# Experts of a gated cross-attention block: the lower part of each weight on VectorE in quarters, GpSimd left with the row additions

## The chip, the cores and the metric

The kernel runs on one core of a Trainium2 chip. The metric is the device time of one execution in microseconds (us). A core has five engines that run their own instruction streams and meet at semaphores: TensorE (PE in the profile; PEld is its weight load), VectorE (DVE), ScalarE (ACT), GpSimd (POOL) and SyncE (SP), which issues DMAs here.

## The reference

The block computes `x + tanh(g) * xattn(layernorm(x))` and then `x + tanh(g) * ffn(layernorm(x))`. The change touches the second, a mixture of experts:

```python
B, S, D, F, E = (4, 512, 256, 1024, 8)           # here x is (8, 512, 256): 4096 tokens
capacity = max(int(N / E * 1.25), 1)              # 640 rows for an expert and a rank
router_probs = softmax(x_flat @ gate_w.T)
top_k_probs, top_k_idx = top_k(router_probs, 2)   # then normalized to a sum of 1
for k in range(2):
    ...
    disp = zeros((E, capacity, D)).at[eid, pos_c].add(where(valid, x_flat, 0))
    gate = silu(einsum('ecd,efd->ecf', disp, wi_gate))
    up = einsum('ecd,efd->ecf', disp, wi_up)
    expert_out = einsum('ecf,edf->ecd', gate * up, wo)
    out = out + where(valid, ew * expert_out[eid, pos_c], 0)
```

## The kernel before, in words

The program has five stages one after the other: `project`, `attend`, `repair`, `route` and `experts`. The first four compute the attention, the router and the rows' places, and write every expert's rows to a buffer in HBM (`scr_disp`). Only `experts` is touched; it runs from about 2475 us to the end of the span.

**Tiling.** The 2 x 640 rows of an expert are 5 chunks of 256 (`NCH` = 5, `R` = 256), 40 chunks in all, counted by `C`; `c` is the chunk within expert `e`. The hidden width F of 1024 is cut in 8 feature blocks of 128 (`FB` = 8).

**Two parts for each number.** TensorE multiplies in fp32r, so every fp32 operand is held as a rounded higher part and a lower part, the difference, and each product is three matmuls: lower x higher, higher x lower, higher x higher (L1467 to L1469). For the rows these are `e_xh` and `e_xl`, for the hidden values `e_hh` and `e_hl`, for the weights `e_wh` and `e_wl`. A weight (gate, up or down: `n` = 0, 1, 2) is 128 x 2048 values; `e_wh` and `e_wl` have two sets, one for the expert that runs and one for the next.

**A chunk, by engine.**
- TensorE transposes the chunk's rows into `e_ps_x` (L1459, 4 transposes), then does `down` of the chunk two before (48 matmuls into `e_ps_y`), then `up` of this chunk: for each feature block 12 matmuls into one of four banks `e_ps_gu`. Block f waits until `e_h` of block f-4 is done, as that frees its bank. Ahead of an expert's first chunk it waits until the three lower parts of its weights are done (`w_cut`).
- ScalarE rounds the rows (`e_xh`), weighs the results of the chunk two before (`e_y`, L1535) and takes tanh of each block (`e_th`).
- VectorE forms `e_xl` (L1546), and for each block `e_sg` (L1578), `e_hh` of the block before (L1551), `e_h` (L1587) and `e_hl` of the block before (L1555). In the last three chunks of an expert it also forms the higher part of one weight of the next, right behind `e_xl` (`high_weight`, L1563). Most of its experts run in a hardware loop over r, two experts an iteration; the other engines' code is unrolled.
- GpSimd adds the weighed rows of chunk `C` to the output with two indirect DMAs (`add_rows`, L1402), and forms the lower part of the weights (`cut_weight`, L1394), one 128 x 2048 subtraction each. The order is written out: chunk by chunk, first `add_rows(C - 2)`, then in the last three chunks of an expert one `cut_weight` for the next.
- SP loads weights into two buffers `e_raw` (`load_weight`, L1426) and rows into four buffers `e_xin` (`load_rows`, L1432). The load of a weight waits until the weight two before it is cut, since that frees the buffer.

Before the first chunk all three weights of expert 0 are loaded, rounded and cut; this is called the head below.

Of the kernel before, what the change touches and what calls it, by code (L numbers as in the profile page):

```python
# [5 lines left out]
F32 = mybir.dt.float32  # L6
# [4 lines left out]
ALU = mybir.AluOpType  # L11
# [3 lines left out]
P = 128  # L15
# [1315 lines left out]
def experts(nc, pl, io, scr, out):  # L1331
# [3 lines left out]
    D, E, F, KD, CAP = pl.D, pl.E, pl.F, pl.KD, pl.CAP  # L1335
    FB = F // P
    RT = 2 if (2 * CAP) % (2 * P) == 0 else 1
    R = RT * P
    NCH = 2 * CAP // R
    DX, XB, LATE = pl.DX, 4, 2  # L1340
    assert CAP % P == 0
    with ExitStack() as ctx:
        sb = lambda name, shape, dt=F32: ctx.enter_context(nc.sbuf_tensor(name, shape, dt))
        psum = lambda name, cols=512: ctx.enter_context(nc.psum_tensor(name, [P, cols], F32))
# [3 lines left out]
        raw = sb("e_raw", [P, 2, KD * F])  # L1348
# [22 lines left out]
        w_high = sem("e_w_high")  # L1371
# [12 lines left out]
        @block.gpsimd  # L1384
        def _(pool):
            nc.gpsimd.memset(ident[:], 0.0).then_inc(id0, 1)
            pool.wait_ge(id0, 1)
            nc.gpsimd.affine_select(out=ident[:], in_=ident[:], compare_op=ALU.not_equal, fill=1.0, base=0,
                                    pattern=[[-1, P]], channel_multiplier=1).then_inc(ident_ready, 1)

            def cut_weight(e, n):
                u = e % 2
                pool.wait_ge(w_high, 3 * e + n + 1)
                nc.gpsimd.tensor_tensor(wl[:, u, n], raw[:, (u + n) % 2], wh[:, u, n].bitcast(F32), ALU.subtract  # L1394
                                        ).then_inc(w_cut, 1)

            def add_rows(C):
                pool.wait_ge(y_sb, RT * (C + 1))
                if C:
                    pool.wait_ge(added, 16 * RT * C)  # L1400
                for r in range(RT):
                    pool.indirect_dma_start(  # L1402
                        out=out.rearrange("b s d -> (b s) d"),
                        out_offset=bass.IndirectOffsetOnAxis(ap=xin[:, C % XB, r, DX - 1:DX].bitcast(U32), axis=0),
                        in_=y[:, C % 2, r, :], in_offset=None, bounds_check=pl.N - 1, oob_is_err=False,
                        compute_op=ALU.add).then_inc(added, 16)

            for n in range(3):
                cut_weight(0, n)
            for C in range(E * NCH):  # L1410
                e, c = divmod(C, NCH)
                if C >= LATE:
                    add_rows(C - LATE)
                if c >= NCH - 3 and e + 1 < E:
                    cut_weight(e + 1, c - NCH + 3)
            for C in range(E * NCH - LATE, E * NCH):
                add_rows(C)
            pool.wait_ge(added, 16 * RT * E * NCH)

        @block.sync  # L1420
        def _(sp):
            def load_weight(e, n):
                u, name = e % 2, ("wgT", "wuT", "wdT")[n]
                if 3 * e + n >= 2:
                    sp.wait_ge(w_cut, 3 * e + n - 1)
                sp.dma_start(raw[:, (u + n) % 2, :].rearrange("p (k f) -> p k f", k=FB if n == 2 else KD),  # L1426
                             io[name][e].rearrange("(k p) f -> p k f", p=P)).then_inc(raw_in[(u + n) % 2], 16)

            def load_rows(C):
                if C >= XB:  # L1430
                    sp.wait_ge(added, 16 * RT * (C - XB + 1))
                sp.dma_start(xin[:, C % XB], scr["disp_c"][C].rearrange("(r p) d -> p r d", p=P)).then_inc(x_in[C % XB], 16)  # L1432

            for n in range(2):
                load_weight(0, n)
            load_rows(0)
            load_weight(0, 2)
            for C in range(E * NCH):
                e, c = divmod(C, NCH)
                if C:  # L1440
                    load_rows(C)
                if e + 1 < E and c == 0:
                    load_weight(e + 1, 0)
                    load_weight(e + 1, 1)
                if e + 1 < E and c == NCH - 1:
                    load_weight(e + 1, 2)

        @block.tensor
        def _(pe):
            pe.wait_ge(ident_ready, 1)  # L1450

            def turn(C, first):

                pe.wait_ge(x_in[C % XB], 16 * (C // XB + 1))
                if not first:
                    pe.wait_ge(x_cut, C)
                for k in range(KD):
                    for r in range(RT):
                        mm = nc.tensor.transpose(ps_x[:, k * R + r * P:k * R + (r + 1) * P],  # L1459
                                                 xin[:, C % XB, r, k * P:(k + 1) * P], ident[:])  # L1460
                mm.then_inc(x_turned, 1)

            def product(out, parts_a, parts_b):

                n = len(parts_a)
                for k, ((ah, al), (bh, bl)) in enumerate(zip(parts_a, parts_b)):
                    nc.tensor.matmul(out, al, bh, start=(k == 0), stop=False)  # L1467
                    nc.tensor.matmul(out, ah, bl, start=False, stop=False)  # L1468
                    mm = nc.tensor.matmul(out, ah, bh, start=False, stop=(k == n - 1))  # L1469
                return mm  # L1470

            def up(C, s, u, start):
                pe.wait_ge(x_cut, C + 1)
                for f in range(FB):
                    n = C * FB + f
                    if not (start and f < 4):
                        pe.wait_ge(h_done, n - 3)
                    for i in range(2):
                        part = [slice(k * F + f * P, k * F + (f + 1) * P) for k in range(KD)]
                        mm = product(ps_gu[f % 4][:, i * R:(i + 1) * R],  # L1480
                                     [(wh[:, u, i, c], wl[:, u, i, c]) for c in part],
                                     [(xh[:, s, k, :], xl[:, s, k, :]) for k in range(KD)])
                    mm.then_inc(gu_full, 1)

            def down(C, s, u, start):
                if not start:
                    pe.wait_ge(y_sb, RT * (C - 1))
                pe.wait_ge(h_cut, (C + 1) * FB)
                for r in range(RT):
                    rows = slice(r * P, (r + 1) * P)  # L1490
                    mm = product(ps_y[s][:, r * D:(r + 1) * D],
                                 [(hh[:, s, f, rows], hl[:, s, f, rows]) for f in range(FB)],
                                 [(wh[:, u, 2, f * D:(f + 1) * D], wl[:, u, 2, f * D:(f + 1) * D]) for f in range(FB)])
                mm.then_inc(y_full, 1)

            def expert(e, u, start):
                pe.wait_ge(w_cut, 3 * e + 3)
                for c in range(NCH):
                    C, q = e * NCH + c, u * NCH + c
                    s = q % 2  # L1500
                    turn(C, start and q == 0)
                    if not (start and q < 2):
                        down(C - 2, s, u if c >= 2 else 1 - u, start and q < 4)
                    up(C, s, u, start and q == 0)

            over(pe, E, 2, expert)
            for q in (2 * NCH - 2, 2 * NCH - 1):
                down((E - 2) * NCH + q, q % 2, 1, False)
# [34 lines left out]
        def _(dve):  # L1543
# [5 lines left out]
            def high(n, s, f):  # L1549
                dve.wait_ge(h_done, n + 1)  # L1550
                nc.vector.tensor_copy(hh[:, s, f, :], h[:, f % 2, :]).then_inc(h_high, 1)  # L1551

            def lower(n, s, f):
                dve.wait_ge(h_high, n + 1)
                nc.vector.tensor_tensor(hl[:, s, f, :], h[:, f % 2, :], hh[:, s, f, :].bitcast(F32), ALU.subtract  # L1555
                                        ).then_inc(h_cut, 1)

            def high_weight(e, u, n, start):
# [3 lines left out]
                    dve.wait_ge(y_full, NCH * (e - 1))  # L1562
                nc.vector.tensor_copy(wh[:, u, n], raw[:, (u + n) % 2]).then_inc(w_high, 1)  # L1563

            def expert(e, u, start, last=False):
                for c in range(NCH):
                    C, q = e * NCH + c, u * NCH + c
                    s = q % 2
                    cut_x(C, s)
                    if c >= NCH - 3 and not last:  # L1570
                        high_weight(e + 1, 1 - u, c - NCH + 3, start and u == 0)
                    for f in range(FB):
                        n = C * FB + f
# [14 lines left out]
                                                       in1=ps_gu[f % 4][:, R:2 * R], op0=ALU.mult, op1=ALU.mult).then_inc(h_done, 1)  # L1588
                        if f:
                            lower(n - 1, s, f - 1)  # L1590
                    high(C * FB + FB - 1, s, FB - 1)
                    lower(C * FB + FB - 1, s, FB - 1)


            for n in range(3):
                high_weight(0, 0, n, True)
            expert(0, 0, True)
            expert(1, 1, True)
            expert(2, 0, False)
# [90 lines left out]
```

## Time and profile before

| what | value |
|---|---|
| three runs | 3287.62 us median (3280.4 to 3288.7) |
| the profiled execution | 3283.47 us, its span 3281.7 us |
| PE busy | 2536.3 us, 77% of the span |
| DVE busy | 2788.9 us, 85% |
| ACT busy | 1460.3 us, 44% |
| POOL busy | 1915.2 us, 58% |
| mean granted TensorE clock | 0.914 of full speed |

Busy times are sums over the whole span, the four earlier stages included. In the rows further down, times are microseconds from the span's start unless a column is named ns; `L` and a number is a line of the kernel; `out<-in` names the tiles that an instruction writes and reads. A duration is the time from an instruction's start to its end; instructions that follow one another on an engine overlap a little, so start to start is shorter than the duration.

### The profile page before, as it was taken

What the parts mean: (1) busy time and instruction counts of PE and PEld (TensorE: products, weight loads), DVE (VectorE), ACT (ScalarE), POOL (GpSimd) and SP (SyncE); (2) the same over time, 40 slices, a digit from 0 to 9 for tenths busy, and PEclk for the clock granted to TensorE, in tenths of its full rate; (3) what the DMA queues carried; (4) which work ended last, traced back from release to release, by engine and by line L of the source; (5) the groups of instructions that cost most, each with busy time, mean ns of one, the idle gap of its engine ahead of it and who ended that gap; (6) DMA issues with size and microseconds to landing.
All of it is one profiled execution on the core that took longest, in us unless ns stands there. A gap on an engine that the chain in (4) does not pass through costs nothing. (4 is left out here: it accounts for less than half of the span.)

```text
span 3281.7 us, 64952 instructions
## 1 busy us (share of the span) xinstructions
PE 2536.3 (77%) x17723; PEld 1599.8 (49%) x17724; DVE 2788.9 (85%) x20206; ACT 1460.3 (44%) x1991; POOL 1915.2 (58%) x1393
## 2 busy tenths in 40 slices
PE   7837787887787778787788778753645999999998
PEld 4512333333333333333333333322544999999998
DVE  6739999999999999999999999956554777777775
ACT  2205666666666666666666666631111222222222
POOL 1017888888888888888888888840163233232231
PEclk9968999999999999999999999985767999999999
DMA  6961211212112112112121121101232222222221
GB/s 189 260 185 31 64 37 31 61 37 45 48 37 64 29 37 64 29 41 59 29 56 45 29 64 37 29 12 41 89 115 93 61 64 62 52 57 62 50 40 20
DMA packets 131053, 201.23 MB, mean 61 GB/s; under 512 B 22816, under 2 KB 97824, under 8 KB 127616
## 3 DMA queue, kind: packets, MB, share of 16 engines
q1 hardware_dynamic: 112768, 167.56, 18.9%
q0 software_dynamic: 17920, 29.52, 4.3%
q8 instruction: 141, 2.31, 0.3%
q14 instruction: 224, 1.84, 0.2%
HBM read 129.60 MB, written 69.50 MB: 61 GB/s over the span
## 5 line engine op out<-in xcount | busy, mean ns | idle before, releaser
L568 DVE MAX8 a_cand<-a_sc 128x8 f32<-128x43 f32 (+1 forms) x12288 | 1646.0, 193 | 50.3 <-ACT a_sc L509 50.2
L670 POOL TENSOR_SCALAR a_side<-a_sc,a_top 128x1024 bf16<-128x1024 f32 x512 | 1455.9, 2844 | 333.1 <-DVE a_top L602 329.4
L509 ACT COPY a_sc<-a_ps_s 128x1024 f32<-128x1024 f32 x512 | 518.3, 1012 | 781.2 <-POOL a_side L670 720.4
L520 ACT ACTIVATE a_pT<-a_ps_e 128x1024 f32<-128x1024 f32 x512 | 526.3, 1028 | 15.2 <-PE a_ps_e L440 11.4
L419 PE MATMUL a_ps_s<-a_ks,a_qs 96*128 96x512 bf16 x1024 | 319.6, 395 | 246.1 <-ACT a_sc L509 192.5
L433 PE MATMUL a_ps_e<-a_qs,a_ks 99*128 99x512 bf16 x1024 | 317.0, 392 | 179.5 <-ACT a_pT L520 178.6
L1402 POOL DMA_INDIRECT out<-e_y,e_xin x80 | 124.0, 1550 | 558.9 <-ACT e_y L1535 516.4
L472 PE MATMUL a_ps_o<-a_pT,a_vs 128*32 128x512 f32 x2048 | 429.0, 693 | 1.1 <-ACT a_pT L520 1.1
L1467 PE MATMUL e_ps_gu<-e_xh,e_wl 128*128 128x256 f32 x1280 | 368.2, 288 | 54.6 <-DVE e_h L1587 49.5
L1468 PE MATMUL e_ps_gu<-e_xl,e_wh 128*128 128x256 f32 x1280 | 365.1, 285 | 0.0
L1469 PE MATMUL e_ps_gu<-e_xh,e_wh 128*128 128x256 f32 x1280 | 364.8, 285 | 0.0
L440 PEld LDWEIGHTS a_ps_e<-a_big,a_side 128*128 128x128 bf16 x4096 | 285.6, 101 | 129.5 <-issue 13.6
L450 PE MATMUL a_ps_c<-a_side,a_row_of 128*16 128x512 bf16 x1024 | 331.5, 408 | 0.0
L440 PE MATMUL a_ps_e<-a_big,a_side 128*128 128x128 bf16 x4096 | 329.6, 226 | 0.0
L419 PEld LDWEIGHTS a_ps_s<-a_ks,a_qs 96*128 96x128 bf16 x1024 | 71.5, 108 | 517.0 <-ACT a_sc L509 341.6
L595 DVE MATCH_REPLACE8 a_cand<-a_top,a_cand 128x24 f32<-128x24 f32 (+2 forms) x1536 | 296.3, 193 | 0.0
L1527 ACT ACTIVATE e_th<-e_ps_gu 128x256 f32<-128x256 f32 x320 | 123.3, 385 | 386.5 <-PE e_ps_gu L1469 268.2
L1578 DVE SCALAR_TENSOR_TENSOR e_sg<-e_th,e_ps_gu 128x256 f32<-128x256 f32 x320 | 133.0, 416 | 185.3 <-ACT e_th L1527 169.9
L1467 PEld LDWEIGHTS e_ps_gu<-e_xh,e_wl 128*128 128x128 f32 x1280 | 246.3, 192 | 59.7 <-DVE e_h L1587 53.7
L433 PEld LDWEIGHTS a_ps_e<-a_qs,a_ks 99*128 99x128 bf16 x1024 | 76.9, 99 | 378.7 <-issue 211.2
L1468 PEld LDWEIGHTS e_ps_gu<-e_xl,e_wh 128*128 128x128 f32 x1280 | 246.5, 193 | 0.0
L1469 PEld LDWEIGHTS e_ps_gu<-e_xh,e_wh 128*128 128x128 f32 x1280 | 246.2, 192 | 0.0
(201 smaller groups left out, 4163.2 us busy)
## 6 DMA issues: line engine op xcount, KB each, us to landing
scr_v<-p_vp SPq DMA_DIRECT2D x32, 512.0 KB, 6.0
a_vs<-scr_v SPq DMA_DIRECT2D x32, 512.0 KB, 5.7
a_mask<-in_mask SPq DMA_DIRECT2D x32, 512.0 KB, 6.6
scr_k<-p_kp SPq DMA_DIRECT2D x96, 128.0 KB, 2.4
a_ks<-scr_k SPq DMA_DIRECT2D x32, 384.0 KB, 4.6
a_qs<-scr_q SPq DMA_DIRECT2D x192, 64.0 KB, 5.2
scr_disp<-a_blank SPq DMA_DIRECT2D x16, 650.0 KB, 8.2
e_xin<-scr_disp SPq DMA_DIRECT2D x40, 260.0 KB, 2.8
```

The source lines that it names most:

```text
L419: mm = nc.tensor.matmul(ps_s[:, h * 512:(h + 1) * 512], qs[0:KR, u, j, qt * P:(qt + 1) * P], ks[0:KR, u, j, h * 512:(h + 1) * 512], start= ...
L433: nc.tensor.matmul(ps_e[:, i * S:(i + 1) * S], ks[:, u, j, keys], qs[:, u, j, :], start=True, stop=False)
L440: mm = nc.tensor.matmul(ps_e[:, i * S + qt * P:i * S + (qt + 1) * P], side[:, (QT * H + qt) % SIDES, keys], big[:], start=False, stop=qt = ...
L450: mm = nc.tensor.matmul(ps_c[0:TILES, :], row_of[:, i, :], side[:, T % SIDES, h * 512:(h + 1) * 512], start=(i == 0 and h == 0), stop=(i = ...
L472: mm = nc.tensor.matmul(ps_o[VW * c:VW * (c + 1), :], vs[:, u, k, VW * j:VW * (j + 1)], pT[:, k, :], start=(half == 0), stop=(half == 1), ...
L509: nc.scalar.copy(sc[:, T % 4, :], ps_s[:]).then_inc(copied, 1)
L520: nc.scalar.activation(pT[:, 2 * n:2 * n + 2, :].rearrange("p k q -> p (k q)"), ps_e[:], ACT.Exp).then_inc(expd, 1)
L568: ins = nc.vector.max(c[:, 8 + n:8 + n + 7 * CH + 1:CH], sc[:, T % 4, pl.cut[n]:pl.cut[n + 1]])
L670: nc.gpsimd.tensor_scalar(side[:, T % SIDES, :], sc[:, T % 4, :], top[:, T // TILES % 2, T % TILES, pl.TOPK - 1:pl.TOPK], None, ALU.is_lt) ...
L1467: nc.tensor.matmul(out, al, bh, start=(k == 0), stop=False)
L1468: nc.tensor.matmul(out, ah, bl, start=False, stop=False)
L1469: mm = nc.tensor.matmul(out, ah, bh, start=False, stop=(k == n - 1))
```

## The change

The subtraction that forms a weight's lower part moves from GpSimd to VectorE and is cut in four (`PIECES` = 4) of 128 x 512 (`PART`). In the last three chunks of each expert but the last, one quarter follows `e_hl` in each of the blocks 1 to 4 (behind `lower(n - 1, ...)`); in the head the four quarters of each weight follow its higher part. `w_cut` now counts quarters, so the waits of SP and TensorE on it are multiplied by four. GpSimd calls `add_rows(C)` in order for all chunks and nothing else.

```diff
-    DX, XB, LATE = pl.DX, 4, 2
-    assert CAP % P == 0
+    DX, XB = pl.DX, 4
+    PIECES = 4
+    PART = KD * F // PIECES
+    assert CAP % P == 0 and FB >= PIECES + 2
...
-            def cut_weight(e, n):
-                u = e % 2
-                pool.wait_ge(w_high, 3 * e + n + 1)
-                nc.gpsimd.tensor_tensor(wl[:, u, n], raw[:, (u + n) % 2], wh[:, u, n].bitcast(F32), ALU.subtract
-                                        ).then_inc(w_cut, 1)
-
...
-            for n in range(3):
-                cut_weight(0, n)
             for C in range(E * NCH):
-                e, c = divmod(C, NCH)
-                if C >= LATE:
-                    add_rows(C - LATE)
-                if c >= NCH - 3 and e + 1 < E:
-                    cut_weight(e + 1, c - NCH + 3)
-            for C in range(E * NCH - LATE, E * NCH):
                 add_rows(C)
...
                 if 3 * e + n >= 2:
-                    sp.wait_ge(w_cut, 3 * e + n - 1)
+                    sp.wait_ge(w_cut, PIECES * (3 * e + n - 1))
...
-                pe.wait_ge(w_cut, 3 * e + 3)
+                pe.wait_ge(w_cut, PIECES * (3 * e + 3))
...
+            def cut_weight(e, u, n, i):
+
+                part = slice(i * PART, (i + 1) * PART)
+                if i == 0:
+                    dve.wait_ge(w_high, 3 * e + n + 1)
+                nc.vector.tensor_tensor(wl[:, u, n, part], raw[:, (u + n) % 2, part], wh[:, u, n, part].bitcast(F32),
+                                        ALU.subtract).then_inc(w_cut, 1)
+
...
-                    if c >= NCH - 3 and not last:
+                    turns = c >= NCH - 3 and not last
+                    if turns:
                         high_weight(e + 1, 1 - u, c - NCH + 3, start and u == 0)
...
                         if f:
                             lower(n - 1, s, f - 1)
+                        if turns and 0 < f <= PIECES:
+                            cut_weight(e + 1, 1 - u, c - NCH + 3, f - 1)
...
             for n in range(3):
                 high_weight(0, 0, n, True)
+                for i in range(PIECES):
+                    cut_weight(0, 0, n, i)
```

## Rows read from the trace of the kernel before

**Rows 1.** The page's slices: PE's busy tenths in 40 equal parts of the span.
```profile
PE   7837787887787778787788778753645999999998
```

**Rows 2.** By tile: line, engine, operation, count, then ns min/median/max, first and last start.
```profile
L1555 DVE TENSOR_TENSOR e_hl<-e_h,e_hh x320: 407/417/6079, 2505.9 to 3260.8; 128x256 fp32r<-128x256 f32 x160
L1551 DVE CAST e_hh<-e_h x320: 275/285/5502, 2505.3 to 3260.5; 128x256 fp32r<-128x256 f32 x160
L1546 DVE TENSOR_TENSOR e_xl<-e_ps_x,e_xh x40: 681/683/692, 2498.4 to 3243.7; 128x512 fp32r<-128x512 f32 x40
L1563 DVE CAST e_wh<-e_raw x24: 1214/1217/4296, 2479.5 to 3154.1; 128x2048 fp32r<-128x2048 f32 x24
L1394 POOL TENSOR_TENSOR e_wl<-e_raw,e_wh x24: 4493/5141/5168, 2480.8 to 3160.4; 128x2048 fp32r<-128x2048 f32 x24
```

**Rows 3.** PE's waits (us, times, longest): from 2470 us, then from 2550 us.
```profile
PE e_ps_gu L1467 <- DVE e_h L1587: 49.5, 21, 2.6
...
PE e_ps_gu L1467 <- DVE e_xl L1546: 1.1, 1, 1.1
```

**Rows 4.** Timeline of one stop: start us, us, instruction, idle before and releaser.
```profile
2830.33 5.79 DVE L1555 TENSOR_TENSOR e_hl<-e_h,e_hh 128x256 fp32r<-128x256 f32 x1
...
2830.67 5.17 POOL L1394 TENSOR_TENSOR e_wl<-e_raw,e_wh 128x2048 fp32r<-128x2048 f32 x1
...
2836.05 0.41 DVE L1578 SCALAR_TENSOR_TENSOR e_sg<-e_th,e_ps_gu 128x256 f32<-128x256 f32 x1
...
2837.05 0.38 PE L1467 MATMUL e_ps_gu<-e_xh,e_wl 128*128 128x256 f32 x1 [2.34 <-DVE e_h L1587]
2837.25 0.41 DVE L1578 SCALAR_TENSOR_TENSOR e_sg<-e_th,e_ps_gu 128x256 f32<-128x256 f32 x1
```

**Rows 5.** Windows of one chunk: us, busy us of each engine, PEclk, DMA share, GB/s.
```profile
2645.01:2665.15 20.14, 17.80 (x151) 17.59 (x149) 17.07 (x35) 4.51 (x11) 7.70 (x3) 1.00 0.33 82
...
2721.65:2743.25 21.60, 19.27 (x150) 19.07 (x149) 16.99 (x34) 4.51 (x11) 7.69 (x3) 0.92 0.31 75
...
2802.51:2820.04 17.53, 17.53 (x151) 17.53 (x149) 11.09 (x34) 4.51 (x11) 3.09 (x2) 1.00 0.15 26
```

**Rows 6.** Chain of work: the transposes that begin the third and the last chunk.
```profile
2527.78 0.44 PE e_ps_x L1459 x4
...
3241.34 0.44 PE e_ps_x L1459 x4
```

**Rows 7.** Timeline of a chunk without a stop.
```profile
2802.35 0.60 PE L1459 MATMUL e_ps_x<-e_ident,e_xin 128*128 128x128 f32 x4
...
2808.48 0.28 PE L1467 MATMUL e_ps_gu<-e_xh,e_wl 128*128 128x256 f32 x1
...
2811.95 0.42 DVE L1578 SCALAR_TENSOR_TENSOR e_sg<-e_th,e_ps_gu 128x256 f32<-128x256 f32 x1 [0.41 <-ACT e_th L1527]
...
2812.15 1.54 POOL L1402 DMA_INDIRECT out<-e_y,e_xin  x1 [0.30 <-issue]
...
2812.82 0.41 DVE L1555 TENSOR_TENSOR e_hl<-e_h,e_hh 128x256 fp32r<-128x256 f32 x1
...
2822.36 0.69 DVE L1546 TENSOR_TENSOR e_xl<-e_ps_x,e_xh 128x512 fp32r<-128x512 f32 x1
```

**Rows 8.** Timeline of the head, before the first chunk.
```profile
2479.48 1.23 DVE L1563 CAST e_wh<-e_raw 128x2048 fp32r<-128x2048 f32 x1 [33.33 <-DMA e_raw<-in_wgT]
...
2485.31 0.37 SPq L1426 DMA_DIRECT2D e_raw<-in_wdT  x1
...
2490.57 1.45 DVE L1563 CAST e_wh<-e_raw 128x2048 fp32r<-128x2048 f32 x1 [4.21 <-DMA e_raw<-in_wdT]
...
2496.69 1.08 PE L1459 MATMUL e_ps_x<-e_ident,e_xin 128*128 128x128 f32 x4 [53.40 <-POOL e_wl L1394]
```

**Rows 9.** Timeline at VectorE's loop back-edge, ahead of chunk 25.
```profile
2982.54 0.69 DVE L1546 TENSOR_TENSOR e_xl<-e_ps_x,e_xh 128x512 fp32r<-128x512 f32 x1 [2.65 <-issue]
```

**Rows 10.** DMA issues in the experts: count, median us from issue to landing.
```profile
out<-e_y,e_xin POOLq DMA_INDIRECT x80, 3.7
```

## The prediction

> **What bounds the kernel now.** The page's slices come first [rows 1]: PE stands at nine tenths from the 32nd slice on, the stretch in which the experts run, and not above it. Who holds it back shows in the rows by tile [rows 2]: the median of `e_hl` (L1555) is 417 ns and its longest is 6079 ns. Its neighbours L1551 and L1394 show the rest: one `e_hh` took 5502 ns, and GpSimd's `e_wl`, the lower part of a weight, takes 5141 ns and occurs 24 times. Next come the waits of PE in the experts [rows 3]: 21 waits for `e_h`, 49.5 us. Then the timeline of one of them [rows 4]: VectorE's `e_hl` starts at 2830.33, GpSimd's `e_wl` at 2830.67 and ends at 2835.84, and `e_hl` ends at 2836.12, 5.4 us longer than its median. All its inputs were there. Meanwhile PE ran through its four banks, sat idle 2.34 us and went on at 2837.05. Of the 24 `e_wl`, the 21 for experts 1 to 7 fall among the chunks, three for each expert, and there are 21 waits: each lower part on GpSimd stops VectorE once.
>
> What a stop costs is read from chunks of 256 rows, from one `e_ps_x` to the next [rows 5]. An undisturbed one takes 17.53 us, all of it PE. With a stop it takes 20.14, or 21.60 where the granted clock averages 0.92: there PE came back at the lower of its two levels (1.2 GHz) after the gap. So in a chunk PE is the limit, and VectorE matters only where it is stopped. From the third chunk to the last, the chain has 37 chunk lengths [rows 6]: 3241.34 - 2527.78 = 713.56 us, and 37 x 17.53 = 648.61. The excess is 64.95 us.
>
> **The change, part by part.**
>
> *GpSimd's `e_wl` goes.* With it the 21 stops go, if nothing else causes them. In the excess there is also one wait that has another cause: at the back-edge of VectorE's loop, `e_xl` starts 2.65 us late on issue [rows 9], and PE waited 1.1 us for it [rows 3]. I take 1.4 us for it with its restart, and leave it in: 64.95 - 1.4 = 63.5 us off. It splits into 49.5 us of idle time and about 14 us that PE ran slower after it.
>
> *VectorE's quarters come.* 24 x 4 subtractions of 128x512 from SBUF. None is in the trace. `e_xl` has the same shape with one operand in PSUM, 683 ns; `e_hl` is 128x256 in SBUF, 417 ns [rows 2], so 256 elements more cost 266 ns, and both ways give 0.68 us. Behind one another `e_hl` and `e_sg` start 0.33 us apart, so a quarter takes 0.33 + 0.27 = 0.60 us of the engine. Bounds: it can't be under the 0.33 us of the half-sized `e_hl`; above stands a quarter of GpSimd's 5.14 us, 1.28 us. I take 0.60, the nearer rows being VectorE's own.
>
> *Do they fit?* A feature block takes VectorE 1.20 us when it doesn't wait (`e_sg` 2836.05 to 2837.25 [rows 4]) and PE 12 matmuls, some 1.42 us. The 0.22 us left don't hold 0.60, so from block 2 on VectorE falls behind by 0.38 us a block, 1.5 us at block 5, and wins 0.2 back in each of the last. What is late next? Three waits of PE, counted from a quiet chunk's start at 2802.35 [rows 7]:
> - Bank reuse: block f+4 needs `e_h` of block f. `e_h` of block 1 is done at 2812.9 (just after `e_hl` starts), block 5 starts five blocks after 2808.48, at 2815.6. The slack is 2.7 us; the last block that counts within a chunk, block 3, is 0.8 us late.
> - `e_xl` of the next chunk: at 2822.36 it starts 2.5 us into a chunk whose first `e_ps_gu` stands at +6.13. It takes 0.7, so the slack is 2.9 us against a lag of some 1.1.
> - The last quarter of an expert's third weight must be done before the next expert's first transpose, at +17.53. Block 1's `e_sg` starts at +9.60; four times 1.20 + 0.60 later it is +16.8, and the end by duration +16.9. The slack is only 0.6 us, in 7 chunks. Bounds: nothing, or at 1.28 us a quarter 4 x 0.68 - 0.6 = 2.1 us each.
>
> So I cost the quarters at nothing: PE's 17.53 us of matmuls cover them.
>
> *`add_rows` moves to its own place.* GpSimd now only waits for `e_y` and issues its two indirect DMAs a chunk; their order against ScalarE and SP stays, since chunk C's rows were ready only in chunk C+2 before as well. In a quiet chunk an `e_hl` of 0.41 us runs inside the indirect DMA of 1.54 us that starts at 2812.15 [rows 7], neither longer than elsewhere. So the DMAs cost VectorE nothing and I take 0, with an upper bound of one such DMA's overlap with the first quarter, 0.6 us, which the bank slack hides.
>
> A rule speaks against this part. The Trainium skill (DMA: Bandwidth & Descriptors, SWDGE vs HWDGE vs iDMA) says that GpSimd writes the descriptors of its DMAs into SBUF and that VectorE locks it out there while it runs in its two-port mode. By that rule the adds could land later beside a busier VectorE. The rows say otherwise so far: 80 issues with the copies `e_hh` beside them, and the one in [rows 7] has its usual length. By the rule the sum would still be the same, as an add lands 3.7 us after its issue [rows 10] and is first awaited two chunks, 35 us, later.
>
> *SP.* The load of an expert's third weight now waits for four counts in place of one, all made in the first turned chunk around +16.9 instead of about +15.8. It is wanted two chunks after that one starts, 18 us later, and lands in 5. Nothing.
>
> *The head.* Before the first chunk the three weights go one by one [rows 8]: the copy at 2479.48, GpSimd's cut, whose end lets the load of the third weight go at 2485.31, its copy at 2490.57 with 1.45 us, its cut, PE at 2496.69. Now the first cut lies on VectorE: 2479.48 + 1.23 + 0.05 + 3 x 0.60 + 0.68 = 2483.24. The third load starts there, lands 5.26 us later at 2488.5, and the second weight is through by then (2483.3 + 1.22 + 2.5 = 2487.0). Copy 1.22, cut 2.53: 2492.3. PE starts 4.4 us earlier. Bounds: 0 and 5.
>
> *Sum:* 63.5 + 4.4 = 67.9 us. The profiled execution took 3283.47 us (its span is 3281.7), which gives 3215.6. The median of the runs shown is 4.1 us above that execution and their lowest 3.1 us below, so I forecast 3218 us for the median.
>
> **The rivals.**
> - *The clock doesn't come back.* If the lower level in chunks such as 2721.65 [rows 5] has another cause than the gap, the 14 us of slower running stay: 3232 us. For it: only some stopped chunks fall to 0.92. Against: the quiet chunks I read are at 1.00.
> - *VectorE becomes late.* At 1.28 us a quarter, `e_xl` is held 4 x 0.68 more than my 1.1, 3.8 against a slack of 2.9: 0.9 us in 14 chunks, and 2.1 us in the 7 where an expert begins: 27 us, 3245 us. A milder form is the third wait alone missing its 0.6 us by up to 1 us: 7 us, 3225.
> - *Slower than before.* The same mechanism, place VectorE's queue between the blocks: with x us a quarter the loss is 14 (4x - 4.2) + 7 (4x - 3.0), and it passes 67.9 us at x = 1.76 us. Then the whole subtraction would take VectorE 7 us, above GpSimd's 5.14. At 2 us the loss is 88 us and the time 3306. Nothing in `e_hl`'s 417 ns speaks for it.
> - *It doesn't do what it says:* the long `e_hl` stem from something else, such as the indirect DMAs. Then only the head is won: 3279, or 3283 for the median. Against it: the stop begins and ends with `e_wl` in [rows 4], and the chunks without `e_wl` have the DMAs but no stop.
>
> The Trainium skill (GPSIMD Engine Reference, Specifications) states that GpSimd shares its SBUF interfaces with VectorE and contends with VectorE instructions that have two SBUF inputs. By it the stop would be one of access and not of order, and the full 21 would go; the copy of 5502 ns, which has one input, would fall under its clause on the two-port mode.
>
> **How the numbers follow.** My forecast 0.72 (its own range 3211 to 3224); the third wait late 0.09; the clock stays 0.08; VectorE late at 3245 0.06; no effect 0.03; slower 0.02. A measurement of this kernel tells about 0.3% from no change, 10 us. Faster by more than that 0.95, within it 0.03, slower 0.02. The range of 8 in 10 reaches from 3210, for a head and a back-edge wait fully won and runs as low as the lowest shown, to 3233, past the clock case.
>
> **What would show it.** After the change no `e_hl` or `e_hh` is over 1 us; the quarters take 0.68 us and follow within 0.60; PE's waits for `e_h` are gone and turned chunks measure 17.5 us at a granted clock of 1.00; the first `e_ps_x` starts near 2492.3; about 1 us of wait for `e_xl` stays at the back-edge. I am wrong if PE waits for quarters or `e_xl` in many chunks, if chunks remain at 0.92, or if VectorE is stopped beside the indirect DMAs.

## The result and the profile after

| | before | after |
|---|---|---|
| runs of the first comparison, median | 3288.16 us (3280.4 to 3289.18) | 3212.95 us (3211.86 to 3217.4) |
| ratio, 95% interval | | 0.9779 [0.9761, 0.9796] |
| the profiled execution, its span | 3283.47, 3281.7 us | 3217.4, 3215.6 us |
| VectorE busy | 2788.9 us | 2730.7 us |
| GpSimd busy | 1915.2 us | 1804.5 us |

The kernel became 2.2% faster. In a second comparison the ratio was 0.9776 [0.9761, 0.979]. One execution of another kernel (`pool_first`, the second time) took 3725 us at a mean granted clock of 0.60 and is left out of every number below. VectorE took over all of the subtraction work and is busy 58 us less: the time it had stood stopped counted as busy.

The tiles of the changed kernel come first, in the columns of [rows 2]: count, then ns min/median/max.

```profile
L1543 DVE TENSOR_TENSOR e_hl<-e_h,e_hh x320: 415/422/438, 2503.2 to 3194.7; 128x256 fp32r<-128x256 f32 x160
L1539 DVE CAST e_hh<-e_h x320: 283/289/334, 2502.6 to 3194.4; 128x256 fp32r<-128x256 f32 x160
L1558 DVE TENSOR_TENSOR e_wl<-e_raw,e_wh x96: 680/691/699, 2482.2 to 3103.6; 128x512 fp32r<-128x512 f32 x96
L1551 DVE CAST e_wh<-e_raw x24: 1216/1219/1227, 2480.9 to 3091.6; 128x2048 fp32r<-128x2048 f32 x24
```

The longest `e_hl` went from 6079 to 438 ns, the longest `e_hh` from 5502 to 334. Read the maxima here, since the medians hardly moved. A quarter has 691 ns. TensorE's waits in the experts answer to [rows 3] (us, times, longest):

```profile
PE e_ps_x L1447 <- DVE e_wl L1558: 48.9, 1, 48.9
PE e_ps_gu L1455 <- DVE e_xl L1534: 5.1, 3, 2.6
```

The line for `e_h`, 49.5 us in 21 waits, is gone. Chunk lengths in the columns of [rows 5]: three in a row, the first two with the quarters in them, the third an expert's first.

```profile
2630.62:2648.14 17.52, 17.52 (x150) 17.52 (x149) 14.12 (x40) 4.51 (x11) 3.10 (x2) 1.00 0.39 91
2648.14:2665.66 17.52, 17.52 (x150) 17.52 (x149) 14.09 (x40) 4.51 (x11) 3.10 (x2) 1.00 0.28 72
2665.66:2683.19 17.53, 17.53 (x151) 17.53 (x149) 12.31 (x39) 4.52 (x11) 3.10 (x2) 1.00 0.43 107
```

All have the full clock and a TensorE that never waits. The chain gives the borders of the 37 chunks, as in [rows 6]:

```profile
2525.48 0.44 PE e_ps_x L1447 x4
...
3175.20 0.44 PE e_ps_x L1447 x4
```

649.72 us, where it was 713.56. The whole account of the two spans, from the first weight load (2474.55 before, 2476.06 after), through the first transpose and these borders:

| stretch | before | after | gained |
|---|---|---|---|
| up to the first weight load | 2474.55 | 2476.06 | -1.5 |
| head, to the first transpose | 22.14 | 17.82 | 4.3 |
| chunks 0 and 1 | 31.09 | 31.60 | -0.5 |
| chunks 2 to 38 | 713.56 | 649.72 | 63.8 |
| last chunk and end | 40.36 | 40.40 | 0.0 |
| span | 3281.7 | 3215.6 | 66.1 |

How the quarters lie in VectorE's time, in the chunk from 2648.14 (start us, us, instruction), and TensorE at its end:

```profile
2657.78 1.55 POOL L1398 DMA_INDIRECT out<-e_y,e_xin  x1 [0.30 <-issue]
...
2658.45 0.42 DVE L1543 TENSOR_TENSOR e_hl<-e_h,e_hh 128x256 fp32r<-128x256 f32 x1
2658.78 0.69 DVE L1558 TENSOR_TENSOR e_wl<-e_raw,e_wh 128x512 fp32r<-128x512 f32 x1
2659.39 0.42 DVE L1575 SCALAR_TENSOR_TENSOR e_sg<-e_th,e_ps_gu 128x256 f32<-128x256 f32 x1
...
2660.58 0.69 DVE L1558 TENSOR_TENSOR e_wl<-e_raw,e_wh 128x512 fp32r<-128x512 f32 x1
...
2664.18 0.69 DVE L1558 TENSOR_TENSOR e_wl<-e_raw,e_wh 128x512 fp32r<-128x512 f32 x1
...
2665.50 0.60 PE L1447 MATMUL e_ps_x<-e_ident,e_xin 128*128 128x128 f32 x4
```

From one quarter to the next are 1.80 us against 1.42 us of matmuls in a block: VectorE falls behind. The last quarter ends at 2664.87 and TensorE needs it at 2665.50, 0.6 us later. The indirect DMA beside the first quarter has its usual 1.55 us, and so have the 80 together (1540 to 1701 ns, median 1548).

### The profile page after: what moved, and what is told of

The parts are those of the page before. It is cut to its first block and busy times, and to the rows that moved or that the text cites. A ratio compares the mean times of both kernels' runs of the same rounds, so it can differ in the third digit from the quotient of the medians.

```text
span 3215.6 us, 65036 instructions
## 1 busy us (share of the span) xinstructions
PE 2518.2 (78%) x17723; PEld 1588.5 (49%) x17724; DVE 2730.7 (85%) x20302; ACT 1460.8 (45%) x1991; POOL 1804.5 (56%) x1369
## 3 DMA queue, kind: packets, MB, share of 16 engines
q14 instruction: 222, 1.82, 0.2%
## 5 line engine op out<-in xcount | busy, mean ns | idle before, releaser
L568 DVE MAX8 a_cand<-a_sc 128x8 f32<-128x43 f32 (+1 forms) x12288 | 1707.6, 210 | 50.2 <-ACT a_sc L509 50.1
L595 DVE MATCH_REPLACE8 a_cand<-a_top,a_cand 128x24 f32<-128x24 f32 (+2 forms) x1536 | 322.6, 210 | 0.0
L602 DVE MAX8 a_top<-a_cand 128x8 f32<-128x80 f32 x1024 | 246.8, 241 | 2.0
```

Source lines behind the costliest of these rows:

```text
L568: ins = nc.vector.max(c[:, 8 + n:8 + n + 7 * CH + 1:CH], sc[:, T % 4, pl.cut[n]:pl.cut[n + 1]])
```

## The experiments

Theory A: a GpSimd instruction on SBUF data shuts VectorE out of `e_hl` and `e_hh` for as long as it runs; the change gains because that no longer falls where VectorE is wanted, and the quarters fit in TensorE's cover. Theory B: the gain comes from another part, the data that the two engines share, the order of the row additions or the smaller load of GpSimd.

**`pool_first`: the same work on GpSimd, earlier.**

```diff
             for C in range(E * NCH):
                 e, c = divmod(C, NCH)
-                if C >= LATE:
-                    add_rows(C - LATE)
                 if c >= NCH - 3 and e + 1 < E:
                     cut_weight(e + 1, c - NCH + 3)
+                if C >= LATE:
+                    add_rows(C - LATE)
```

> The kernel before, with one change: GpSimd does cut_weight ahead of add_rows in a chunk, so its 5.1 us subtraction starts when the higher part is there (about +4.2 us into a chunk) and not behind the two indirect DMAs (+10.6). Theory A (GpSimd's subtraction shuts VectorE out while VectorE wants an instruction with two SBUF inputs or a fast copy; what costs is when it happens): from +4.2 to about +9 VectorE sits idle or runs e_sg and e_h with PSUM operands, its first e_hh is at +9.8, so the 21 stops and PE's 49.5 us of waits for e_h go without any work for VectorE: 63.5 us off, about 3224 us; the head stays at 22.1 us from the first load to the first transpose. Theory B (the gain came from somewhere else in the change, the order of the row additions or less work on GpSimd): 3283 to 3288 us, stops stay.

Measured: 3218.22 us, ratio 0.9796 [0.9773, 0.9819]; repeated beside the changed kernel, 3218.56 us, ratio 0.9788 [0.9773, 0.9802], against 3214.26. Two lines moved, and nearly all of the gain is there with no quarter on VectorE. The time is 6 us under the 3224 expected. The 37 chunks take 648.5 us, 65 less than before and not 63.5, as the wait at the back-edge is gone too. The head stayed at 22.1 us, as expected. A chunk of it:

```profile
2616.20 1.22 DVE L1563 CAST e_wh<-e_raw 128x2048 fp32r<-128x2048 f32 x1
2617.50 4.60 POOL L1394 TENSOR_TENSOR e_wl<-e_raw,e_wh 128x2048 fp32r<-128x2048 f32 x1 [10.57 <-DVE e_wh L1563]
...
2621.28 0.42 DVE L1578 SCALAR_TENSOR_TENSOR e_sg<-e_th,e_ps_gu 128x256 f32<-128x256 f32 x1 [3.87 <-ACT e_th L1527]
2621.79 0.42 DVE L1587 SCALAR_TENSOR_TENSOR e_h<-e_sg,e_ps_gu 128x256 f32<-128x256 f32 x1
2622.25 1.55 POOL L1402 DMA_INDIRECT out<-e_y,e_xin  x1 [0.15 <-issue]
```

The subtraction runs from 2617.50 to 2622.10, in the time in which VectorE waits for `e_th`. `e_sg` and `e_h` run beside it at their usual 0.42 us: they have one operand in PSUM. So where GpSimd's work lies is what counts. Theory B fails for the order of the additions too, which go later here.

**`pool_quarters`: GpSimd's subtraction in four.**

```diff
-                nc.gpsimd.tensor_tensor(wl[:, u, n], raw[:, (u + n) % 2], wh[:, u, n].bitcast(F32), ALU.subtract
-                                        ).then_inc(w_cut, 1)
+                for i in range(4):
+                    part = slice(i * KD * F // 4, (i + 1) * KD * F // 4)
+                    op = nc.gpsimd.tensor_tensor(wl[:, u, n, part], raw[:, (u + n) % 2, part],
+                                                 wh[:, u, n, part].bitcast(F32), ALU.subtract)
+                op.then_inc(w_cut, 1)
```

> The kernel before, with GpSimd's subtraction cut in four of 128x512, at its old place. Theory A with a lock that lasts one GpSimd instruction: VectorE's e_hl or e_hh is stopped up to four times for about 1.2 us each instead of once for 5.4, the lag is nearly the same, PE still waits about 2 us in 21 chunks: 3270 to 3288 us. Rival (the lock can be shared fairly, VectorE gets in between elements or instructions and keeps pace): longest e_hl under 1 us, 3225 us.

Measured: 3310.52 us, ratio 1.0084 [1.0053, 1.0116], slower than before and outside both expectations. The timeline of a stop:

```profile
2637.12 6.16 DVE L1558 TENSOR_TENSOR e_hl<-e_h,e_hh 128x256 fp32r<-128x256 f32 x1
2637.43 5.55 POOL L1396 TENSOR_TENSOR e_wl<-e_raw,e_wh 128x512 fp32r<-128x512 f32 x4
...
2644.20 0.39 PE L1470 MATMUL e_ps_gu<-e_xh,e_wl 128*128 128x256 f32 x1 [2.71 <-DVE e_h L1590]
```

I had expected one stop for each quarter. A single `e_hl` stood through all four: GpSimd's instructions, one behind another, gave VectorE no turn in between, and the stop grew from 5.79 us to 6.16. Over the 37 chunks TensorE is idle 8.4 us more than before and busy 12.9 us more, and 13 of the chunks have a granted clock under 0.95, where 6 had it before. So pieces one right behind another don't help; pieces on GpSimd with something else between them were not tried.

**`dummy_sub` and `dummy_copy`: GpSimd busy beside the changed kernel.**

```diff
+            for j in range(2):
+                nc.gpsimd.memset(idle[:, j], 0.0).then_inc(idle_set, 1)
+            pool.wait_ge(idle_set, 2)
             for C in range(E * NCH):
-                add_rows(C)
+                e, c = divmod(C, NCH)
+                if C >= 2:
+                    add_rows(C - 2)
+                if c >= NCH - 3 and e + 1 < E:
+                    pool.wait_ge(w_high, 3 * e + 3 + c - NCH + 3 + 1)
+                    e_n = 3 * e + c - NCH + 3
+                    pool.wait_ge(idle_set, 2 + e_n)
+                    nc.gpsimd.tensor_tensor(idle[:, 2], idle[:, 0], idle[:, 1], ALU.subtract).then_inc(idle_set, 1)
+            for C in range(E * NCH - 2, E * NCH):
+                add_rows(C)
```

In `dummy_copy` the operation is `tensor_copy(idle[:, 2], idle[:, 0])`.

> The changed kernel, with a subtraction of 128x2048 from and to scratch tiles of its own put on GpSimd at the old place and moment; nothing reads its result. Theory A (GpSimd running beside VectorE is the cause): 21 stops of e_hl of 5 to 6 us come back, and as the quarters now lie behind them PE waits about 3 us in 14 chunks and 5 us in the 7 that end an expert, with the lower clock after some: 3290 to 3305 us. Theory B (the stop came from the data that the two engines share, or from who waits for w_cut): 3213 us, no e_hl over 1 us.

> The same with a copy (one SBUF input) on GpSimd in place of the subtraction. Theory A1 (any GpSimd instruction on SBUF data shuts VectorE out for its whole length): stops as long as the copy runs; with 2.5 us or more PE waits up to 1 us a chunk, 3213 to 3235 us. Theory A2 (only a GpSimd instruction with two inputs does): 3213 us and no e_hl over 1 us.

Measured, one execution each: 3313.22 us and 3244.42 us. The stops, and what GpSimd ran, first with the subtraction:

```profile
2635.27 5.76 DVE L1557 TENSOR_TENSOR e_hl<-e_h,e_hh 128x256 fp32r<-128x256 f32 x1
2635.60 5.14 POOL L1417 TENSOR_TENSOR e_idle<-e_idle 128x2048 f32<-128x2048 f32 x1
```

and with the copy:

```profile
2625.62 3.09 DVE L1557 TENSOR_TENSOR e_hl<-e_h,e_hh 128x256 fp32r<-128x256 f32 x1
2625.94 2.49 POOL L1417 COPY e_idle<-e_idle 128x2048 f32<-128x2048 f32 x1
```

There are 21 stops in each (20 of `e_hl` and one of a quarter). With tiles that nobody else touches the stop is the same, 5.76 us against 5.79 in [rows 4]. TensorE waited 61.9 us for `e_h` in 21 waits. That settles theory B's shared data: GpSimd's running is enough. The copy has one input, takes 2.49 us and stops `e_hl` for 3.09: the stop follows the length of GpSimd's instruction, whatever its kind of the two. The times are 8 and 9 us above what was expected. In the 37 chunks TensorE's matmuls take 648.6 us at full clock. In `dummy_sub` it is busy 683.7 us, with a granted clock under 0.95 in 15 chunks. In `dummy_copy` it is busy 662.3 us though every chunk has 1.00, so there the clock is not the reason; what it is stays open.

The Trainium skill (SBUF — State Buffer, Who interferes with whom) says that VectorE and GpSimd take a shared pair of ports for a whole instruction, and that VectorE wants it with two SBUF inputs or in its two-port modes, not with at most one SBUF input outside these modes. The runs here agree for `e_hl`, which is stopped for 5.4 us, and for `e_sg`, with one SBUF and one PSUM input, which is not. `e_hh`, stopped once for 5.2 us, has one input and falls under that rule only by a two-port mode; no row names its mode. The Trainium skill says there too that whoever issues first gets the pair. The head of the kernel before agrees: the copy of the second weight started 1.28 us behind GpSimd's subtraction and ended 1.09 us behind it, 3.1 us longer than its usual 1.22.

```profile
2480.79 4.49 POOL L1394 TENSOR_TENSOR e_wl<-e_raw,e_wh 128x2048 fp32r<-128x2048 f32 x1 [5.58 <-DVE e_wh L1563]
2482.07 4.30 DVE L1563 CAST e_wh<-e_raw 128x2048 fp32r<-128x2048 f32 x1 [1.36 <-DMA e_raw<-in_wuT]
```

In the chunks, though, `e_hl` was first by 0.3 us by the recorded starts and still the one that stood; what these starts mean for the lock stays open.

**`whole`: one instruction on VectorE in place of four** (`PIECES = 1`).

> The changed kernel with one subtraction of 128x2048 on VectorE behind block 1 in place of four quarters. By the slack of 2.7 us that I counted for e_h of a block, VectorE's 2.2 us at once still fit (block 2 is 2.0 us late): same time within 0.1%, 3213 us, no waits of TensorE for e_h. Rival (the quarters are needed, the slack is smaller than counted): TensorE waits for e_h up to 1 us in 21 chunks, 3220 to 3235 us.

Measured: 3215.5 us, ratio 0.9785 [0.977, 0.98]. The subtraction takes 2285 ns, TensorE never waits for `e_h`, and every chunk from the third on but the one at the back-edge lasts 17.5 us. The quarters aren't needed: 2.3 us at once fit in the bank slack.

**`twice` and `thrice`: more work in a quarter.**

```diff
-                nc.vector.tensor_tensor(wl[:, u, n, part], raw[:, (u + n) % 2, part], wh[:, u, n, part].bitcast(F32),
-                                        ALU.subtract).then_inc(w_cut, 1)
+                for again in range(3):
+                    if again:
+                        dve.wait_ge(w_cut, 3 * (PIECES * (3 * e + n) + i) + again)
+                    nc.vector.tensor_tensor(wl[:, u, n, part], raw[:, (u + n) % 2, part],
+                                            wh[:, u, n, part].bitcast(F32), ALU.subtract).then_inc(w_cut, 1)
...
-                    sp.wait_ge(w_cut, PIECES * (3 * e + n - 1))
+                    sp.wait_ge(w_cut, 3 * PIECES * (3 * e + n - 1))
...
-                pe.wait_ge(w_cut, PIECES * (3 * e + 3))
+                pe.wait_ge(w_cut, 3 * PIECES * (3 * e + 3))
```

In `twice` it is 2 in place of 3.

> The changed kernel with every quarter done three times over, each repeat behind a wait on the one before, so a quarter takes VectorE about 1.9 to 2.1 us in place of 0.60. My formula 14 (4x - 4.2) + 7 (4x - 3.0) gives 80 to 97 us of loss, and with that no gain over the kernel before: 3293 to 3310 us, the waits at e_xl and at an expert's first transpose. Rival (the price of VectorE's work isn't its overflow over the slack; VectorE's queue costs from the first quarter on, or catches up elsewhere): far outside, 3213 or over 3330 us.

> The changed kernel with every quarter done twice, the second behind a wait on the first: about 1.33 us of VectorE a quarter (three took 2.05). My formula gives 14 (4 x 1.33 - 4.2) + 7 (4 x 1.33 - 3.0) = 32 us of loss in the chunks, and the head 9 us: 3254 us on the median of 3213. Theory (the formula prices the overflow, and adds nothing for the clock): waits of TensorE for e_xl of about 1.1 us in 14 chunks and for the last quarter of about 2.3 us in 7, none for e_h. Rival (as in the kernel with three, the clock falls after the waits and adds a third or more to them): 3265 us or more.

Measured, one execution each: 3350.81 us for `thrice` and 3256.87 us for `twice`. In `twice` a quarter takes VectorE 1.33 us (2632.76 to 2635.29, less the 1.20 of a block). The waits of TensorE over one expert (us, times, longest), from 2620 to 2700 us:

```profile
PE e_ps_x L1447 <- DVE e_wl L1561: 2.2, 1, 2.2
PE e_ps_gu L1455 <- DVE e_xl L1534: 1.8, 2, 0.9
```

The formula gave 2.3, and 1.1 twice. The stage from the third to the last transpose took 684.95 us, 36.3 over 37 x 17.53, where 32 were predicted, without the back-edge, whose chunk is 1.9 us too long. The time is 3 us above the 3254 expected. The rival, a clock that adds a third or more, did not come: one chunk of the 37 has a granted clock under 0.95. With three, a quarter takes 2.05 us, the formula gives 92 us, and the stage lost 121.3: the time is 41 us above the range expected, on the rival's side (over 3330). The waits over one expert and its window, 2622 to 2728 us:

```profile
PE e_ps_gu L1455 <- DVE e_xl L1534: 5.5, 2, 2.8
PE e_ps_x L1447 <- DVE e_wl L1561: 3.9, 1, 3.9
PE e_ps_gu L1455 <- DVE e_h L1587: 2.6, 3, 0.9
```

```profile
2622.30:2727.70 105.40, 93.46 (x741) 92.23 (x740) 81.31 (x204) 22.12 (x55) 17.08 (x10) 0.95 0.23 53
```

An expert takes 105.4 us instead of 87.6, 17.8 more, about 125 for seven. The idle time in the three rows is 12.0 us, 84 for seven, and TensorE is busy 93.46 us for the matmuls that take 87.6 at full clock: 5.9 us, 41 for seven, at a granted clock of 0.95. (Summed over the 37 chunks themselves, 82.1 us idle and 39.3 us busy.) So the formula is near for the waits in sum, 84 against its 92 (those for `e_h` are not in it), and has no term for the slower matmuls behind them; in the kernel before these were 14 us beside 49.5.

In `twice` and `thrice` VectorE is so late that its copy of a weight falls beside GpSimd's indirect DMA. In `twice`:

```profile
2646.54 1.22 DVE L1551 CAST e_wh<-e_raw 128x2048 fp32r<-128x2048 f32 x1
2647.42 1.76 POOL L1398 DMA_INDIRECT out<-e_y,e_xin  x1 [14.12 <-ACT e_y L1523]
2649.49 1.55 POOL L1398 DMA_INDIRECT out<-e_y,e_xin  x1 [0.30 <-issue]
```

and in `thrice`, where most of these copies take longer as well:

```profile
2668.67 2.40 POOL L1398 DMA_INDIRECT out<-e_y,e_xin  x1 [15.24 <-ACT e_y L1523]
2669.56 1.43 DVE L1551 CAST e_wh<-e_raw 128x2048 fp32r<-128x2048 f32 x1
```

Of the 80 indirect DMAs 14 lie beside such a copy in each kernel. They take 1.74 to 1.82 us in `twice` and 2.28 to 2.41 in `thrice`; the median of the others is 1.55, beside quarters and `e_hh` too. In the kernels before and after none lies there.

**`head`, `best` and `best2`: where more is to be had.** All three start chunk 0 when gate and up are cut, and round and cut the down weight within it. `head` does that alone on the changed kernel; its change on TensorE:

```diff
-                pe.wait_ge(w_cut, PIECES * (3 * e + 3))
+                if e:
+                    pe.wait_ge(w_cut, PIECES * (3 * e + 3))
...
                     turn(C, start and q == 0)
+                    if C == 0:
+                        pe.wait_ge(w_cut, PIECES * 2)
+                    if C == 2:
+                        pe.wait_ge(w_cut, PIECES * 3)
```

`best` has this head, with VectorE's three cuts in one instruction each, on top of `pool_first`. `best2` also loads the rows of chunk 1 ahead of expert 1's weights:

```diff
             load_weight(0, 2)
+            load_rows(1)
             for C in range(E * NCH):
                 e, c = divmod(C, NCH)
-                if C:
+                if C > 1:
                     load_rows(C)
```

> The changed kernel with the head alone altered as in best: e_xl of chunk 0 formed between the first two weights, TensorE's first chunk waiting for two weights, the third rounded and cut in chunk 0. Theory: 7 us less than the changed kernel, 3206 us, and about 1 us more than best, which has no wait at the back-edge. Rival: given back in chunks 0 to 2, 3212 us.

> Neither way alone: GpSimd keeps the cuts of experts 1 to 7 and does them ahead of the row additions (as in pool_first), VectorE does the three of the head in one instruction each, and TensorE starts the first chunk when gate and up are cut, with the down weight rounded and cut during chunk 0. From the traces: chunks at 17.52 us with no wait at the loop's back-edge (pool_first has none, the changed kernel 1.1 us); first e_ps_gu at about 2489.2 on the changed kernel's clock where it was 2496.4, 7 us earlier. Theory A: 3213 - 1 - 7 = 3205 us. Rival (the head's end is set by rows or by the down weight, so an early start is given back in chunks 0 to 2): 3212 us.

> The kernel best with one move on SP: the rows of chunk 1 are loaded ahead of the two weights of expert 1, whose second waits for the third cut. Theory (TensorE's wait for e_xin in chunk 1, 1.2 us in best and 5 us in head, came from that queue): the wait goes, 3209 us at 3210 for best. Rival (the wait is hidden by e_xl of chunk 1 anyway): same as best within 0.3 us in the trace.

Measured: `head` 3216.26 us, ratio 0.9786 [0.9773, 0.98]; `best` 3210.14 us, 0.9768 [0.9755, 0.9782]; `best2` 3208.84 us, 0.9763 [0.9749, 0.9778], and beside it the changed kernel again 3214.26. `head` is above both the 3206 us expected and its rival's 3212; `best` lies 5 us above its 3205, nearer to its rival's 3212. In the traces the stage from the first weight load to the last chunk's transpose takes 699.14 us in the changed kernel, 698.98 in `head`, 693.78 in `best` and 693.82 in `best2`. The gain of `head` was given back in chunk 1: its rows are queued on SP behind a weight load that waits for the third cut, which now comes late, and TensorE waited 5.0 us for `e_xin`. `best` wins 5.4 us, and the move of that load in `best2` took away the rest of this wait and won nothing, as the rival said. In `best`:

```profile
2503.58 0.66 PE L1457 MATMUL e_ps_x<-e_ident,e_xin 128*128 128x128 f32 x4 [0.98 <-DMA e_xin<-scr_disp]
2506.41 0.39 PE L1465 MATMUL e_ps_gu<-e_xh,e_wl 128*128 128x256 f32 x1 [2.17 <-DVE e_xl L1549]
```

and in `best2`, where the first wait of 1.0 us is gone and the second has grown by 1.3:

```profile
2503.67 0.39 PE L1466 MATMUL e_ps_gu<-e_xh,e_wl 128*128 128x256 f32 x1 [3.49 <-DVE e_xl L1550]
```

In this stage both are 5.4 us ahead of the changed kernel, and by the medians `best2` is 5.4 us (0.17%) ahead of the one beside it. `best` was not run beside it; its median is 3 to 4 us under the two of the changed kernel.

**`pool_first_again` and `after_again`: the pair side by side.**

> The kernel pool_first once more, beside the changed kernel on the same chip. Theory (its head is 4.3 us longer, its back-edge wait of 1.1 us is absent, nothing else differs): 3.2 us more than the changed kernel, ratio to before 0.001 higher.

> The changed kernel once more, beside pool_first and best2 on the same chip: 3213 to 3217 us, ratio to before between 0.977 and 0.980, chunk stage from the third to the last transpose 649.7 us as in its first profile.

Measured: 3218.56 and 3214.26 us, 4.3 apart, where 3.2 were expected; the stages in the traces, from the first weight load to the last chunk's transpose, are 701.96 and 699.04 us, 2.9 apart. The changed kernel took 649.62 us from the third to the last transpose, as expected.

## Why the prediction was right

- *21 stops gone, 63.5 us*: 63.8. Both halves came back, the 49.5 us of idle time and the 14 us of slower matmuls; every chunk that had a stop now runs at 1.00. The rival by which the lower clock had another cause is refuted, and `thrice` shows the other direction, waits and with them a clock of 0.95. That rival was priced too high, as not all of the 14 us is the clock's. A chunk with a stop at a granted clock of 1.00 is busy 17.8 us too, 0.27 over a quiet one; the six at 0.92 are busy 19.1 to 19.4 us, which makes about 8.6 us more in all.
- *A quarter takes 0.68 us and 0.60 of the engine*: 0.69, and 0.60 by the starts (2658.78 to 2659.39).
- *It fits, with 0.6 us to spare at an expert's end*: 0.63 us (2664.87 to 2665.50). `whole`, `twice` and `thrice` put numbers on the slack; the break-even of 1.76 us a quarter is too high, because the formula omits the slower matmuls. With 36 us lost at 1.33 and 121 at 2.05, a line between the two puts the end of the 68 us won near 1.6, an estimate.
- *The indirect DMAs cost nothing*: their median is 1548 ns, as before (1549), and they land 3.8 us after their issue, where it was 3.7. The Trainium skill's rule on locked-out descriptor writing would not have changed the sum. The traces agree with it where a weight's copy falls beside such a DMA, which is 0.2 us longer in `twice` and up to 0.9 us in `thrice`. The prediction had tested it on `e_hh` alone, beside which the DMAs have their usual length; in the changed kernel the copy ends before they begin.
- *The head, 4.4 us*: 4.3.
- *The back-edge, left in*: it stayed.

```profile
2934.98 0.69 DVE L1534 TENSOR_TENSOR e_xl<-e_ps_x,e_xh 128x512 fp32r<-128x512 f32 x1 [2.99 <-issue]
...
2935.73 0.39 PE L1455 MATMUL e_ps_gu<-e_xh,e_wl 128*128 128x256 f32 x1 [1.07 <-DVE e_xl L1534]
```

The issue stall is 2.99 us and TensorE waits 1.07 of it. In `pool_first`, where VectorE isn't behind by the quarters, the stall is 2.65 us and no chunk is longer than 17.7 us: without the lag it is covered.

The forecast for the median, 3218 us, is 5 us above the measured 3212.95. Two small things were missed. The profiled execution came out at 3217.4 us where the sum for it said 3215.6: the stages before the experts took 1.5 us more, and chunks 0 and 1 0.5. And the medians lie 75 us apart, the profiled executions 66. Over all comparisons the kernel before ran from 3277.8 to 3293.2 us and the changed one from 3211.9 to 3217.4. The wider spread would fit a number of slow-clock chunks that differs from run to run (6 of the 21 in the profiled one), which each cost 1.3 to 1.7 us more. The granted clocks on record lean that way: on average 0.913 in the eight executions of the kernel before that took under 3285 us, and 0.910 in the seven over 3290. No second trace of it was taken, so that stays open.

## What to carry to other kernels

When an instruction's median is short and its maximum long, look in the timeline for what GpSimd runs in the same microseconds before looking for a wait: a stopped VectorE instruction counts as busy and has no releaser. The cure need not be to move the work: putting GpSimd's instruction into a gap of VectorE, or beside its PSUM operands, gave all but 3 to 5 us of the same gain for two moved lines. When work is added between the steps of a loop, count the slack of every consumer to the end of the pipeline (bank, next chunk, next expert), and add the slower matmuls that follow once TensorE begins to wait: here 14 us beside 49.5 of waiting, and 39 beside 82 in `thrice`.

## What the runs showed of the hardware

- A stop isn't divided by dividing GpSimd's instruction: four of 128x512 held one `e_hl` for 6.16 us, one of 128x2048 for 5.79.
- GpSimd's 128x2048 subtraction took 5.14 us beside a stopped `e_hl` and 4.58 on average in `pool_first`, where VectorE was idle or read PSUM. In the head it took 4.49 with the copy of a weight stopped beside it, so a stopped instruction alone isn't what lengthens it; what does stays open.
- VectorE's copy of a weight, 1.22 us, and GpSimd's indirect DMA, 1.55 us, lengthen each other where they meet: to 1.76 us for the DMA that started near the copy's end (`twice`), to 1.43 and 2.40 where the DMA started first (`thrice`).
- A GpSimd copy of 2.49 us stops VectorE as its subtraction does, for 2.67 us (3.09 less the usual 0.42).
- VectorE does the same subtraction in 2.29 us, half of GpSimd's time.
